# Cross-attention on one Trainium2 core: scores formed transposed in float32, block maxima of the quadrants joined and spread by small copies on VectorE

## The reference

```python
a = _layer_norm(ctx, gamma, beta)
Q = (x @ Wq.T)   # (B, 16, 112, 32)
K = (a @ Wk.T)   # (B, 16, 375, 32)
V = (a @ Wv.T)   # (B, 16, 375, 32)
scores = einsum('bhtd,bhsd->bhts', Q, K) * 32 ** -0.5
scores = where(mask, scores, -inf)
attn = softmax(scores, axis=-1)
out = einsum('bhts,bhsd->bhtd', attn, V) -> (B, 112, 512)
return x + tanh(gate) * (out @ Wo.T)
```

## Time and profile before

| | us |
|---|---|
| median of 3 runs | 1139.86 (1137.56 to 1142.44) |
| span of the profiled execution | 1134.9 |
| TensorE busy in it | 1100.3 |
| VectorE busy | 861.4 |
| ScalarE busy | 679.0 |
| GpSimd busy | 565.0 |

### The profile page before, as it was taken

How to read it: one execution, slowest core, us unless ns; L and a number is a source line. 1 busy time by engine, 2 the same in 40 slices (tenths; PEclk the granted TensorE clock), 3 DMA queues, 4 the chain that set the end, 5 groups by cost and what they waited for, 6 DMA issues and landing times.

```text
span 1134.9 us, 28841 instructions
## 1 busy us (share of the span) xinstructions
PE 1100.3 (97%) x9614; PEld 921.6 (81%) x9614; DVE 861.4 (76%) x2438; ACT 679.0 (60%) x1811; POOL 565.0 (50%) x745
## 2 busy tenths in 40 slices
PE   9799899999999999999999999999999999999997
PEld 8798788878888888888888888888888887888885
DVE  4643888887877788888787788888787778887764
ACT  2414565656666666666666666666666666666653
POOL 1344746555555566655455566655554566655100
PEclk9899899999999999999999999999999999999997
DMA  9453223222333233323333333323333333331000
GB/s 270 168 152 70 69 73 72 55 76 74 83 85 85 72 85 73 66 64 75 77 85 85 80 77 77 70 56 75 77 85 85 82 75 76 67 67 45 10 17 17
DMA packets 53010, 89.55 MB, mean 79 GB/s; under 512 B 15184, under 2 KB 35664, under 8 KB 52976
## 3 DMA queue, kind: packets, MB, share of 16 engines
q1 hardware_dynamic: 52400, 88.19, 31.8%
q10 hardware_dynamic: 576, 0.92, 0.3%
HBM read 81.66 MB, written 7.44 MB: 79 GB/s over the span
## 4 chain that ended last, share of the span: by engine, by line
PE 72%; DVE 16%; DMA 5%; issue 4%; POOL 1%; ACT 1%; SPq 1%; DVEq 0%; POOLq 0%
PE bank L690 43%; PE bank L747 14%; PE bank L847 6%; DVE shared_f L668 6%; PE bank L770 6%; DVE stats L574 4%; DVE shared_f L649 3%; PE bank L712 2%; DMA qT<-in_wkT 2%; DMA row_stats<-row_stat 1%; DMA rows<-in_ctx 1%; DVE mv L577 1%; POOL cn L404 1%; ACT shared_f L513 1%; DMA stat_bc<-row_stats 0%
## 5 line engine op out<-in xcount | busy, mean ns | idle before, releaser
L404 POOL TENSOR_TENSOR cn<-cn,stat_bc 128x375 f32<-128x375 f32 x256 | 258.8, 1043 | 387.4 <-DMA stat_bc<-row_stats 371.1
L513 ACT ACTIVATE shared_f<-shared_f,ntop 112x375 f32<-112x375 f32 x512 | 306.3, 601 | 14.3 <-DVE ntop L649 14.1
L690 PE MATMUL bank<-shared_r,w_k 128*128 128x376 f32 x1536 | 295.9, 342 | 0.0
L690 PE MATMUL bank<-w_v,shared_r 128*125 128x512 f32 x1152 | 291.7, 402 | 0.1
L649 DVE CUSTOM_DVE_ANT_0 shared_f<-bank,mask_b 112x375 f32<-112x375 f32 x512 | 258.6, 543 | 32.1 <-PE bank L770 30.8
L690 PEld LDWEIGHTS bank<-shared_r,w_k 128*128 128x128 f32 x1536 | 260.4, 190 | 0.3
L747 PEld LDWEIGHTS bank<-ident,shared_f 112*125 112x125 f32 x1536 | 199.1, 190 | 67.9 <-issue 27.9
L690 PEld LDWEIGHTS bank<-w_v,shared_r 128*125 128x125 f32 x1152 | 206.7, 186 | 46.1 <-issue 0.5
L668 DVE TENSOR_SCALAR shared_f<-shared_f,rden 112x375 f32<-112x375 f32 x512 | 240.3, 531 | 4.5
L747 PE MATMUL bank<-ident,shared_f 112*125 112x112 f32 x1536 | 222.1, 281 | 20.2 <-DVE shared_f L668 19.6
L536 ACT ACTIVATE shared_f<-bank 125x448 f32<-125x448 f32 x256 | 139.0, 543 | 166.8 <-PE bank L747 166.8
(11 more groups left out here) (49 smaller groups left out, 816.4 us busy)
## 6 DMA issues: line engine op xcount, KB each, us to landing
rows<-in_ctx SPq DMA_DIRECT2D x32, 750.0 KB
cn<-in_ctxT SPq DMA_DIRECT2D x32, 750.0 KB, 12.2
stat_bc<-row_stats SPq DMA_DIRECT2D x32, 375.0 KB, 4.4
xy<-in_x SPq DMA_DIRECT2D x32, 224.0 KB, 2.5
out<-xy SPq DMA_DIRECT2D x32, 224.0 KB, 2.3
shared_f<-in_xT SPq DMA_DIRECT2D x7, 896.0 KB, 8.9
mask_u<-in_mask SPq DMA_DIRECT2D x32, 41.0 KB, 3.1
qT<-in_wqT SPq DMA_DIRECT2D x4, 256.0 KB, 5.5
```

Source lines behind the costliest of these rows:

```text
L404: last = pool.tensor_tensor(chunk, chunk, stat_bc[:, w, :], op)
L513: last = act.activation(prob[0:T, r % 2, h, :], prob[0:T, r % 2, h, :], ACT.Exp, bias=ntop[0:T, r % 2, h:h + 1], scale=-1.0, accum_out=den ...
L690: last = pe.matmul(dst, l, m, start=(start and k == 0), stop=(stop and k == len(pairs) - 1))
```

## The change

The scores are now formed transposed: context rows on the partitions (three chunks of 125), queries of four heads along the row (448 elements). The softmax weights come out in the layout that the weighted sum reads, and no transposes of weights are left. What changes, engine by engine:

- **TensorE**: scores as 12 plain float32 products a slot (3 chunks x 4 heads, 32 x 125 weights, 112 columns); the 12 transposes go; the weighted sum stays, one slot later; four products with a 32-column block of ones give the sums of the weights. K is projected one slot ahead, the output one batch item later; V and output alternate between two banks. The mask is transposed once for all.
- **ScalarE**: three evictions of scores (125x448, from four banks, mask as bias), eviction of the weighted sum together with the sums, K as one float32 copy, the high part of the output once a batch item, and three exponentials of 125x448 without sums.
- **VectorE**, each slot: three maxima of 128x448 with a 32x32 block transpose on the way in (`quadrant_maxima`); three copies of 32x42 that bring the other quadrants' maxima to the first, and one maximum over 12 of them (`row_maximum`); three copies of 32x14 back to the other quadrants and one transpose of a repeated 128x14 to 128x448 (`spread_maximum`); three subtractions of 125x448 in place. Each of these steps waits for the one ahead through a semaphore. Once a batch item: maximum with transpose, reciprocal, transpose and product of 128x448 (`normalise`), and the low part of the output. The old maxima, scalings, evictions and low parts of K go.
- **GpSimd**: two additions of 125x448 a slot, for the sums (`sum_chunks`); the queries are copied, no longer split; the mask's work shrinks to 125x3 a batch item; the normalisation is spread over three slots (`center`, `divide`, `affine`) and the row statistics go in the fourth.
- **SyncE**: one mask load in all; the other transfers keep their sizes, at other places in the order. Results are stored one batch item later.

```diff
@@ scores, TensorE
-                    for k, (a, d) in enumerate(PASSES):
-                        for h in range(HC):
-                            last = pe.matmul(bank[h][0:T, 0:SE], qr[rows, c, a, u, :], kT[rows, q, d, :],
-                                             start=(k == 0), stop=(k == len(PASSES) - 1))
+                for j in range(ST):
+                    for h in range(HC):
+                        part = slice(HD * h, HD * h + HD)
+                        last = pe.matmul(bank[h][0:SP_, T * j:T * j + T],
+                                         kT[part, r % 2, SP_ * j:SP_ * j + SP_],
+                                         qs[part, c % 2, u, :], start=True, stop=True)
@@ weighted sum, TensorE
+                if old:
+                    pe.wait_ge(sum_done, i * LOOP + (r - 2))
+                    for h in range(HC):
+                        last = pe.matmul(bank[PB][HD * h:HD * h + HD, T:2 * T], ones[0:SP_, :],
+                                         psum[0:SP_, T * h:T * h + T], start=True, stop=True)
@@ ScalarE
+                for j in range(ST):
+                    act.activation(prob[0:SP_, (r - 1) % NB, j, :].rearrange("p (h t) -> p h t", h=HC),
+                                   sbank[0:SP_, :, T * j:T * j + T], ACT.Identity,
+                                   bias=mask_b[0:SP_, c % 2, j:j + 1]).then_inc(s_out, 1)
...
+                    for j in range(ST):
+                        act.wait_ge(sub_done, i * (LOOP * ST) + ((r - 2) * ST + j + 1))
+                        act.activation(prob[0:SP_, (r - 2) % NB, j, :], prob[0:SP_, (r - 2) % NB, j, :],
+                                       ACT.Exp, scale=SCALE).then_inc(exp_done, 1)
@@ VectorE
+            def quadrant_maxima(i, r):
+                for j in range(ST):
+                    dve.wait_ge(s_out, i * (LOOP * ST) + ((r - 1) * ST + j + 1))
+                    last = dve.tensor_reduce(
+                        x4[:, BLK * j:BLK * j + BLK],
+                        prob[:, (r - 1) % NB, j, :].rearrange("p (k a) -> p k a", a=32),
+                        AX.X, ALU.max, apply_transpose=True)
+                last.then_inc(quad_max, 1)
+            def row_maximum(i, r):
+                dve.wait_ge(quad_max, i * LOOP + r)
+                for q in range(1, HC):
+                    last = dve.tensor_copy(x4[0:32, ST * BLK * q:ST * BLK * (q + 1)],
+                                           x4[32 * q:32 * q + 32, 0:ST * BLK])
+                last.then_inc(gathered, 1)
+                dve.wait_ge(gathered, i * LOOP + r)
+                dve.tensor_reduce(top[0:32, :], x4[0:32, :].rearrange("p (a k) -> p k a", k=BLK),
+                                  AX.X, ALU.max).then_inc(top_done, 1)
+            def spread_maximum(i, r):
+                dve.wait_ge(top_done, i * LOOP + r)
+                for q in range(1, HC):
+                    last = dve.tensor_copy(top[32 * q:32 * q + 32, :], top[0:32, :])
+                last.then_inc(top_spread, 1)
+                dve.wait_ge(top_spread, i * LOOP + r)
+                dve.transpose(spread.rearrange("p (k a) -> p k a", a=32),
+                              top[:, :].unsqueeze(2).to_broadcast([128, BLK, 32])) \
+                    .then_inc(spread_done, 1)
+            def subtract_maximum(i, r):
+                dve.wait_ge(spread_done, i * LOOP + r)
+                for j in range(ST):
+                    dve.tensor_tensor(prob[0:SP_, (r - 1) % NB, j, :], prob[0:SP_, (r - 1) % NB, j, :],
+                                      spread[0:SP_, :], ALU.subtract).then_inc(sub_done, 1)
@@ VectorE, the order of a slot
+                if live(i, LOOP, r - 1, SLOTS):
+                    quadrant_maxima(i, r)
+                    row_maximum(i, r)
+                    spread_maximum(i, r)
+                    subtract_maximum(i, r)
+                if u == 3 and live(i, 2, c - 1, B):
+                    normalise(i, c - 1)
...
                 if not early(i, r):
                     context_lo(i, r)
+                if u == 1 and live(i, 2, c - 2, B):
+                    result(i, c - 2)
@@ GpSimd, the order of a slot
+                if u == 3 and live(i, 2, c + 1, B):
+                    copy_q(i, c + 1)
+                    if behind(i, 2, c + 1):
+                        copy_bias(i, c + 1)
+                if live(i, LOOP, r - 3, SLOTS):
+                    sum_chunks(i, r)
+                if u == 0 and live(i, 2, c + 2, B) and not first_two(i, c + 2):
+                    center(i, c + 2)
+                if u == 1 and live(i, 2, c + 2, B) and not first_two(i, c + 2):
+                    divide(i, c + 2)
+                if u == 2 and live(i, 2, c + 2, B) and not first_two(i, c + 2):
+                    affine(i, c + 2)
+                if u == 3 and live(i, 2, c + 4, B) and behind(i, 2, c + 2):
+                    row_statistics(i, c + 4)
```

More of the change, by code:

```diff
@@ new lines, in project_k @@
+            def project_k(i, r):
+                c, u = divmod(r + 1, KT)
+                if u == 0:
+                    pe.wait_ge(c_done, i * LOOP + (c + 1) * KT)
+                    pe.wait_ge(pad_done, 1 if first_two(i, c) and c % 2 == 0 else 2)
+                    pe.wait_ge(w_done, 3 * KT)
+                if behind(i, LOOP, r + 1):
+                    pe.wait_ge(k_done, i * LOOP + (r + 1))
+                product(bank[KB][:, 0:SE],
+                        [(wk[:, a, k, 128 * u:128 * u + 128], cT[:, c % 2, d, k, :])
+                         for k in range(KT) for a, d in PASSES]).then_inc(k_mm, 1)
@@ new lines, in output, with scores @@
+            def output(i, r):
+                c = r // KT - 2
+                pe.wait_ge(o_done, i * 2 + (c + 1))
+                if live(i, 2, c + 2, B):
+                    pe.wait_ge(v_done, i * (2 * ST) + ((c + 2) * ST + 2))
+                else:
+                    pe.wait_ge(y_done, i * 2 + c)
+                product(bank[VO[1]][0:T, :],
+                        [(oT[:, a, k, :], wo[:, d, k, :])
+                         for k in range(KT) for a, d in PASSES]).then_inc(y_mm, 1)
+            def scores(i, r):
+                c, u = divmod(r, KT)
+                if u == 0:
+                    pe.wait_ge(qs_done, i * 2 + (c + 1))
+                pe.wait_ge(k_done, i * LOOP + (r + 1))
+                if behind(i, LOOP, r):
+                    pe.wait_ge(s_out, i * (LOOP * ST) + r * ST)
+                for j in range(ST):
[4 more added lines that the diff above has]
+                                         qs[part, c % 2, u, :], start=True, stop=True)
+                last.then_inc(s_mm, 1)
@@ new lines, in weighted_sum, with transpose_mask, slot @@
+                last.then_inc(pv_mm, 1)
+            def transpose_mask():
+                pe.wait_ge(mask_f_done, 1)
+                pe.wait_ge(q_out, GROUPS * KT)
+                for j in range(ST):
+                    last = pe.transpose(bank[PB][0:SP_, B * j:B * j + B],
+                                        mask_f[0:B, SP_ * j:SP_ * j + SP_], ident[0:B, 0:B])
+                last.then_inc(mask_mm, 1)
+            def slot(i, r):
+                if live(i, LOOP, r + 1, SLOTS):
+                    project_k(i, r)
+                vc, j = v_item(r)
+                if j is not None and live(i, 2, vc, B):
+                    project_v(i, r, vc, j)
+                if r % KT == 1 and live(i, 2, r // KT - 2, B):
+                    output(i, r)
+                if is_slot(i, r, -1):
+                    transpose_mask()
+                if live(i, LOOP, r, SLOTS):
+                    scores(i, r)
+                if live(i, LOOP, r - 2, SLOTS + 1):
+                    if is_slot(i, r, 2):
+                        pe.wait_ge(mask_out, 1)
+                    weighted_sum(i, r)
@@ L855, in _ @@
+            pe.wait_ge(q_out, (GROUPS - 1) * KT + 2)
             slots(pe, slot)
```

604 lines of the change are left out of this document (295 added, 309 removed).

## The result

The changed kernel takes 1371.2 us (median of 4 runs, 1363.2 to 1372.64) against 1138.99 us in the same series: ratio 1.2016, 95% interval 1.1976 to 1.2056. It is 20% slower. I forecast slower, 1225 us, 7.5%; the range ended at 1340.

What follows compares the result with a forecast made beforehand. TensorE bounded the old kernel; VectorE, delayed by GpSimd, was to bound the new one. 128 slots of 8.55 us make 1094, plus 126 around them a 1220 us span, about 1225 us as measured; range 1085 to 1340 us.

Steps and rivals of the forecast that it cites:

- the sum without stops: VectorE's work undisturbed by GpSimd: 5.94 us a slot plus 5.53 us a batch item, 29.3 us a batch item.
- small copies: VectorE's three 42-element and three 14-element copies a slot: 0.17 us each, 1.02 us together before any GpSimd delay.
- the 168-element maximum: VectorE's maximum between the two groups of copies in each slot: 0.34 us.
- GpSimd's train: GpSimd's run of additions and normalisation operations, about 6.3 us a slot, expected to delay VectorE by 4.9 us a batch item.
- the stops: Time VectorE's operations lose waiting for GpSimd's: +4.9 us a batch item, raising 29.3 to 34.2 us, 8.55 a slot.
- my signs of being right: VectorE over 85%, copies well over 0.17 us, subtractions over 0.62, TensorE under 90% at full clock, slots near 8.55 us.
- The first: Rival: VectorE's small copies do not wait for GpSimd and TensorE stays the bound; 1091 us, chance 0.25.
- The second: Rival: GpSimd's operations meet every VectorE chain in full, copies two to six each waiting 0.85 us; 1334 us, chance 0.15.
- The third: Rival: TensorE's float32 scores with 125-column weights cost as much as transposes, 8.6 us a slot; 1232 us, chance 0.08.
- The fourth: Rival: TensorE waits so much that its clock falls from 2.4 to 1.2 GHz; over 1800 us, chance 0.02.

## Why the prediction was wrong

**The bound and the sum without stops were right.** VectorE was to become the bound with 29.3 us a batch item and 1069 us in all; 1081 were found. By term: three transposing maxima 1.68 (1.70 said), small copies 0.173 and 0.165 with 13 ns between (0.17), the 168-element maximum 0.43 (0.34 said, the largest miss), spreading transpose 0.645 (0.62), subtractions 1.70 (1.70). The Trainium skill, "VectorE: DVE Perf Modes", section "Two Vector instructions with no wait between them", had said that instructions changing quadrant are held until the ones ahead have ended: the trace agrees, the three copies stand 0.19 apart, not 0.08.

**The step that failed is the one that laid GpSimd's train against VectorE's chain**: "It starts when the exponentials of a slot are done, 0.7 us after VectorE's last subtraction". I priced the stops at 4.9 us a batch item, 157 us; they were 290, 9.1 a batch item. Their places were wrong too. I gave the copies about 4 of the 4.9 and the subtractions 0.3; measured are 1.9 and 5.1, and 2.0 for low parts and product where I had 0.5. Two things were left out. First, the train starts 6.2 to 8.0 us after the last subtraction of the scores that it adds up (the table above). In three slots of four the exponentials end 1.9 to 5.0 us after that subtraction and not 0.7, as ScalarE's fixed order puts evictions ahead of them that wait for TensorE or for the division. And `sum_chunks` also waits for TensorE's product with ones of the slot before, because there is one `psum` buffer: that alone is 4.9 us in one slot and 0.6 to 1.2 in the others. So the train leaves the maxima, where it does no harm, and lies on the subtractions and what follows. No run gives the sums a second buffer or ScalarE another order; what each delay is worth stays open. Second, a two-input operation on VectorE that meets a train is not stopped once in a group but each time. I had read +0.5 for four subtractions from the earlier trace rows, where GpSimd's operations had one input, and put 0.3 into the sum; against two-input additions three subtractions took 4.24 us for 1.70. The rows for that were there: the scalings of the earlier trace rows show the same alternation. The experiment with later additions shows that the time of the meeting alone is worth 88 us. Most of my signs of being right came true all the same: VectorE at 91%, copies over 0.17 us, TensorE at 80%. The signs told of the stops, and not of their size; only the slot, 9.6 us for 8.55, and TensorE's clock, 0.871 and not full, did not fit.

**Rivals.** The first, copies that do not wait, is refuted: with scores in PSUM they took 597 ns. The second came nearest in size (1334 us) by luck, as its place was wrong: the copies have 61 of the 290 us of stops. The third is wrong: the scores take 0.85 us a slot, not 1.42 nor 2.5, and TensorE needs about 6.8 us a slot when it has no wait. The fourth did happen in part, but TensorE had time to spare. TensorE of the changed kernel in order of time, two slots:

```profile
518.00 0.92 PE L872 MATMUL sbank<-shared_f 32*125 32x112 f32 x24
518.85 0.78 PE L890 MATMUL bank<-shared_f 125*32 125x112 f32 x24
519.45 0.38 PE L897 MATMUL bank<-shared_f,ones 125*32 125x112 f32 x8
519.75 2.33 PE L773 MATMUL bank<-shared_r,w_k 128*128 128x376 f32 x12
521.92 2.96 PE L773 MATMUL bank<-w_v,shared_r 128*125 128x512 f32 x12
524.81 0.92 PE L872 MATMUL sbank<-shared_f 32*125 32x112 f32 x24
...
535.86 1.53 PE L890 MATMUL bank<-shared_f 125*32 125x112 f32 x24 [3.33 <-ACT shared_f L591]
537.17 0.60 PE L897 MATMUL bank<-shared_f,ones 125*32 125x112 f32 x8
537.70 4.13 PE L773 MATMUL bank<-shared_r,w_k 128*128 128x376 f32 x12
```

From 518.00 to 524.81 the slot is 6.8 us without a wait. Behind a wait of 3.33 us the same products take 1.6 to 2 times as long. The windows view of those K products and of the slot before's (PE, PEld, DVE, ACT, POOL busy; then the granted clock):

```profile
526.57:528.89 2.32, 2.32 (x17) 2.32 (x14) 2.29 (x3) 0.92 (x2) 1.75 (x2) 1.00 0.32 130
537.70:541.83 4.13, 4.13 (x16) 3.63 (x12) 4.05 (x6) 1.75 (x4) 3.67 (x3) 0.50 0.00 0
```

The granted clock of the second is 0.50, which is 1.2 GHz; that of the first is 1.00, 2.4 GHz. What the Trainium skill says in "SBUF — State Buffer", section "SBUF: two separate sides", that a VectorE operation with two SBUF inputs competes with a GpSimd operation that reads SBUF for a port that is held for the whole instruction, is borne out: with two inputs in SBUF the subtraction takes 1042 ns in the mean of the changed kernel, and with one in PSUM it is never stopped (616 to 618 ns in four kernels, the longest 626). My second rival applied that rule to the copies alone; what it gives with all the operations that it names was not worked out.

**Where the expected gain went.** TensorE lost its transposes: its slot came down from 7.78 us to about 6.8. That gain was real and off the path, as VectorE's undisturbed 30 us a batch item lies above 27. Against the 31.7 of the kernel before even this would have been 5% faster (1081 against 1139); the stops turned it into 20% slower.

## What to carry to other kernels

Before work is moved to GpSimd, list VectorE's instructions that read two SBUF tensors or copy inside SBUF, and see which of them GpSimd's long operations will meet: each meeting costs up to a whole GpSimd operation, again for each instruction in a row. Putting one operand in PSUM, making a small copy as a maximum over one element, or giving a small sum to a TensorE with time left takes the meeting away; moving GpSimd's start takes away part of it. For the place of the meeting, take every wait of the moved instruction from the diff, buffer reuse included, and the place of its inputs in the fixed order of the engine that writes them.

## What the runs showed that I had not expected

- A 32x14 copy made as a maximum over one element takes 159 ns, less than the copy proper undisturbed (165), and is never stopped.
- A 128x448 float32 block transpose takes 645 ns into SBUF and 660 into PSUM. The maximum with a block transpose on the way in takes 610 ns in the mean, no more than the plain 448-element copy's 620.
- Twelve float32 products over 32 rows with 125-column weights, 24 instructions, take 0.85 us at full clock, 0.036 each. The weighted sum's 24, over 125 rows with 32-column weights, take 0.60, 0.025 each.
